# Expert outputs scattered to the tokens' slots during the expert loop, and a re-ordered attention stage

## What is computed

```
# layer 1, feed-forward: 32 experts, the best 4 for each token, capacity C = 2*1024*4/32 = 256 rows each
flat_ids, flat_w = top-4 experts and weights of each token
pos   = rank of the row within its expert
buf   = zeros(E, C, D).at[expert, pos].set(x[tok], mode='drop')     # rows past the capacity are dropped
eo    = (silu(buf @ gate) * (buf @ up)) @ w2
out_slots = eo[expert, pos]           # a position past the end reads the expert's last row, C-1
routed    = zeros.at[tok].add(out_slots * w)
# layer 2, attention: 32 heads of width 8, q and k normalised, softmax(q k / sqrt 8) v
```

## Time and profile before

| | |
|---|---|
| median of 3 runs | 1113.56 us (1111.15 to 1117.43) |
| the profiled execution | 1113.5 us |
| its span, first to last instruction | 1111.7 us |
| mean granted clock of TensorE | 0.881 of 2.4 GHz |
| busy: PE, DVE, ACT, POOL | 881.0, 649.1, 513.7, 372.0 us |

### The profile page before, as it was taken

The page is one execution under the profiler, slowest core; times in us unless marked ns, Lnnn a source line. Parts: engine busy times, 40 slices in busy tenths (PEclk is TensorE's granted clock), DMA queues, the critical chain, the costliest instruction groups (busy, mean ns, idle before and its releaser), DMA issues. The chain is left out here.

```text
span 1111.7 us, 17091 instructions
## 1 busy us (share of the span) xinstructions
PE 881.0 (79%) x6296; PEld 549.6 (49%) x6296; DVE 649.1 (58%) x1333; ACT 513.7 (46%) x881; POOL 372.0 (33%) x334
## 2 busy tenths in 40 slices
PE   4784689995504888467899898977888899999997
PEld 2334445654303666344555454544545555555554
DVE  4968634448742877244543557854768665754443
ACT  2554533442202888223445854356345777533332
POOL 3977223331379000363023475210135432400000
PEclk9785599998656999777856999989989999999999
DMA  9422044421024888321002345210145544533332
GB/s 324 168 71 69 1 122 130 130 84 42 10 99 137 289 269 291 129 75 39 1 1 85 92 140 182 86 44 29 30 146 160 150 129 138 175 100 100 100 100 81
DMA packets 56798, 126.44 MB, mean 114 GB/s; under 512 B 6921, under 2 KB 18569, under 8 KB 56722
## 3 DMA queue, kind: packets, MB, share of 16 engines
q1 hardware_dynamic: 45442, 108.65, 31.4%
q0 software_dynamic: 3072, 8.39, 2.4%
q10 hardware_dynamic: 8208, 8.39, 2.2%
HBM read 82.90 MB, written 42.50 MB: 113 GB/s over the span
## 5 line engine op out<-in xcount | busy, mean ns | idle before, releaser
L1403 PE MATMUL ps<-turned_buf,wb 128*128 128x512 f16 x576 | 136.5, 388 | 7.5 <-POOL wb L741 7.5
L1403 PE MATMUL ps<-turned_buf,W 128*128 128x512 f16 x576 | 136.9, 389 | 6.4 <-POOL W L741 4.2
L2122 DVE SCALAR_TENSOR_TENSOR ctx_sb<-ps,ctx_sb 128x512 f32<-128x512 f32 x96 | 66.3, 691 | 118.8 <-PE ps L1403 75.7
L1009 ACT ACTIVATE ctxT<-ctx_sb 128x512 f16<-128x512 f32 x96 | 60.3, 629 | 113.9 <-DVE ctx_sb L2122 113.9
L738 POOL TENSOR_SCALAR W<-W 128x768 f32<-128x768 f32 x32 | 69.0, 2155 | 127.9 <-ACT wb L1021 75.7
L2129 DVE TENSOR_TENSOR ctxT<-ctx_sb,ctxT 128x512 f16<-128x512 f32 x96 | 68.3, 712 | 64.0 <-ACT ctxT L1009 63.6
L1001 ACT ACTIVATE ctx_sb<-ps 128x512 f32<-128x512 f32 x96 | 57.2, 596 | 85.6 <-PE ps L1403 85.3
L1403 PEld LDWEIGHTS ps<-turned_buf,wb 128*128 128x128 f16 x576 | 55.9, 100 | 71.4 <-POOL wb L741 9.1
L1403 PEld LDWEIGHTS ps<-turned_buf,W 128*128 128x128 f16 x576 | 55.9, 100 | 71.3 <-issue 7.6
L1346 PE MATMUL ps<-turned_buf,W 128*128 128x512 f16 x360 | 88.2, 399 | 2.4 <-issue 2.4
L1419 PE MATMUL ps<-wb,ctxT 128*128 128x256 f16 x576 | 71.7, 275 | 10.8 <-DVE ctxT L2129 6.6
(11 more groups left out here) (378 smaller groups left out, 1800.6 us busy)
## 6 DMA issues: line engine op xcount, KB each, us to landing
W<-in_w SPq DMA_DIRECT2D x79, 384.0 KB, 3.7
kept<-W SPq DMA_DIRECT2D x24, 384.0 KB, 4.2
kept<-wb SPq DMA_DIRECT2D x24, 384.0 KB, 4.3
W<-kept SPq DMA_DIRECT2D x24, 384.0 KB, 3.0
wb<-kept SPq DMA_DIRECT2D x24, 384.0 KB, 3.1
seats<-wq ACTq DMA_DIRECT2D x1, 8192.0 KB, 37.8
arena<-seats SPq DMA_DIRECT2D x32, 256.0 KB, 3.8
served<-arena SPq DMA_DIRECT2D x32, 256.0 KB, 2.7
```

The costliest lines, as they stand in the source:

```text
L1009: nc.scalar.activation(h_16[:, g % 2, 0, :], h_g[:, g % 2, :], ACT.Copy).then_inc(sem("h_hi"), 1)
L1403: last = nc.tensor.matmul(bank(4 + n), w4[k % 4][:, w, n * D + c * P:n * D + (c + 1) * P], x16[:, i, c, half * HALF:(half + 1) * HALF], st ...
L2122: nc.vector.scalar_tensor_tensor(h_g[:, g % 2, :], bank(5), 1.0 / WSCALE, h_s[:, g % 2, :], ALU.mult, ALU.mult).then_inc(sem("gated"), 1)
```

## The change

1. `seats` rows get 32 more columns (ROW = 288), and the normalised rows are scattered with them. VectorE writes there, for each token and expert, a number from which the row's slot (token, order among its four) follows: a running count (`m_cum`) plus the partition's base, times "has a seat".
2. During the expert loop POOL reads from `e_x` the column of expert k, makes slot numbers `m_dest`, waits for `e_y(k)` and scatters its 256 rows with two indirect DMAs into `slots` (4096 rows in DRAM). SP's loads of rows wait for `e_dest` as well. SP no longer stores the outputs; it copies each expert's last row to `last_rows`.
3. After the loop SP loads `slots` with 8 plain DMAs into four buffers `e_back`. What had no seat is added by one more product per tile: the transposed weights of those picks (`over_T`) times `last_rows`.
4. The diagonals move from POOL to VectorE. `seats` and `slots` are set to zero later, by two DMAs from ScalarE's queue behind the conversion of the router's weights.
5. Before unit 0 all four sums and two pairs' queries are made, on more PSUM banks; pairs 2 and 3 follow at n = 3 and 11. 32 dummy products stand before the first sum, and one in each of the units 13 to 41.
6. FIRST_UNIT is 42, with three half steps per four units (18 beside the units, 14 behind), and the preparation of layer 2's experts moves ahead accordingly. q2_norm fuses two operations into one, three times.

The diff, cut to its core:

```diff
+ROW = D + E1
+SLOTS = T * TOP1
...
-        xn = sb("xn", [P, B, D])
+        x_rows = sb("xn", [P, B, ROW])
+        xn = x_rows[:, :, 0:D]
...
-        bkv3 = sb("bkv3", [1, 2 * D])
+        bkv3 = wq2[0:1, :, :].rearrange("p k d -> p (k d)")
...
-        seats = nc.dram_tensor("seats", (E1 * CAPACITY, D), F32, kind="Internal").ap()
-        served = nc.dram_tensor("served", (E1 * CAPACITY, D), F32, kind="Internal").ap()
+        seats = nc.dram_tensor("seats", (E1 * CAPACITY, ROW), F32, kind="Internal").ap()
+        slots = nc.dram_tensor("slots", (SLOTS, D), F32, kind="Internal").ap()
...
-        e_x = ar.take([3, CT, D])
+        m_w = ar.take([B, TOP1])
+        m_dest = ar.take([3, CT]).bitcast(U32)
+        e_x = ar.take([3, CT, ROW])
...
-        ar.at = at_back = ARENA - (2 * TOP1 * D + 2 * B * TOP1)
-        e_back = ar.take([2, TOP1, D])
-        m_from = ar.take([B, TOP1]).bitcast(U32)
-        m_w = ar.take([B, TOP1])
+        ar.at = at_back = ARENA - 4 * TOP1 * D
+        e_back = ar.take([4, TOP1, D])
...
-        FIRST_UNIT = 50
+        FIRST_UNIT = 42
+        REST = (8 * B + 2 - FIRST_UNIT) * 3 // 4
+        Q_TURN = (3, 11)
+        Q_PRODUCT = (4, 12)
+        Q_NORM = (1, 8, 19)
+        Q_SCALE = (2, 9, 20)
+        Q_LOW = (3, 5, 10, 13, 21, 23)
...
+        def steps_at(n):
+
+            return range(max(n - FIRST_UNIT, 0) * 3 // 4, max(n + 1 - FIRST_UNIT, 0) * 3 // 4)
...
-            sp.wait_ge(sem("seats_zero"), 16)
+            sp.wait_ge(sem("kv_mm"), 2 * B)
...
                 if k >= 3:
                     sp.wait_ge(sem("e_turn"), k - 2)
+                    sp.wait_ge(sem("e_dest"), k - 2)
                 sp.dma_start(e_x[:, k % 3, :, :], seats[k * CAPACITY:(k + 1) * CAPACITY, :].rearrange("(p c) d -> p c d", c=CT))\
...
-            def expert_store(k):
+            def last_row(k):
 
                 sp.wait_ge(sem("e_y"), k + 1)
-                sp.dma_start(served[k * CAPACITY:(k + 1) * CAPACITY, :].rearrange("(p c) d -> p c d", c=CT), e_y[k % 3])\
-                    .then_inc(sem("served", k % 3), 16)
+                sp.dma_start(last_rows[k:k + 1, :], e_y[k % 3][P - 1:P, CT - 1, :]).then_inc(sem("last", k % 3), 16)
+
+            def back(t):
+
+                if t >= 4:
+                    sp.wait_ge(sem("back_read"), t - 3)
+                sp.dma_start(e_back[:, t % 4, :, :].rearrange("p i d -> p (i d)"),
+                             slots.rearrange("(p k) d -> p (k d)", p=P)[:, t * TOP1 * D:(t + 1) * TOP1 * D])\
+                    .then_inc(sem("back", t % 4), 16)
...
-                        expert_store(k - 2)
+                        last_row(k - 2)
                 for k in range(E1 - 2, E1):
-                    expert_store(k)
+                    last_row(k)
+                for i in range(3):
+                    sp.wait_ge(sem("last", i), 16 * len(range(i, E1, 3)))
+                    sp.wait_ge(sem("served", i), 16 * CT * len(range(i, E1, 3)))
+                for t in range(B):
+                    back(t)
...
-            nc.gpsimd.memset(wq2[:, 0, :], 0.0).then_inc(sem("set_up"), 1)
...
+                nc.gpsimd.memset(k_norm[:, 0:2, :, :].rearrange("p k b h -> p (k b h)"), 0.0).then_inc(sem("set_up"), 1)
...
-            pool.wait_ge(sem("seats_zero"), 16)
+            pool.wait_ge(sem("seats_zero"), 16 * 2)
             pool.wait_ge(sem("seat"), 2)
             for t in range(B):
                 for i in range(TOP1):
                     nc.gpsimd.indirect_dma_start(seats, bass.IndirectOffsetOnAxis(ap=m_to[:, t, i:i + 1], axis=0),
-                                                 x_rms[:, t, :], None, bounds_check=E1 * CAPACITY - 1, oob_is_err=False)\
+                                                 x_rows[:, t, :], None, bounds_check=E1 * CAPACITY - 1, oob_is_err=False)\
                         .then_inc(sem("seated"), 16)
-            pool.wait_ge(sem("seat"), 4)
-            pool.wait_ge(sem("a1_pv"), 2)
-            for t in range(B):
-                for i in range(TOP1):
-                    ins = nc.gpsimd.tensor_scalar(diag(t, i), ident[:, :], m_w[:, t, i:i + 1], None, ALU.mult)
-            ins.then_inc(sem("back_diag"), 1)
-            for i in range(3):
-                pool.wait_ge(sem("served", i), 16 * len(range(i, E1, 3)))
-            for t in range(B):
-                if t >= 2:
-                    pool.wait_ge(sem("back_read"), t - 1)
-                for i in range(TOP1):
-                    nc.gpsimd.indirect_dma_start(e_back[:, t % 2, i, :], None, served,
-                                                 bass.IndirectOffsetOnAxis(ap=m_from[:, t, i:i + 1], axis=0),
-                                                 bounds_check=E1 * CAPACITY - 1, oob_is_err=False)\
-                        .then_inc(sem("back", t % 2), 16)
-                    if i == 1 and t in (2, 5):
-                        inv_sqrt_pair(t // 2 - 1 if t == 2 else 1)
+            for k in range(E1):
+                pool.wait_ge(sem("ex_in", k % 3), 16 * (k // 3 + 1))
+                if k >= 3:
+                    pool.wait_ge(sem("served", k % 3), 16 * CT * (k // 3))
+                nc.gpsimd.tensor_scalar(m_dest[:, k % 3, :], e_x[:, k % 3, :, D + k], -1.0, NOWHERE, ALU.mult, ALU.add)\
+                    .then_inc(sem("e_dest"), 1)
+                pool.wait_ge(sem("e_dest"), k + 1)
+                pool.wait_ge(sem("e_y"), k + 1)
+                for c in range(CT):
+                    nc.gpsimd.indirect_dma_start(slots, bass.IndirectOffsetOnAxis(ap=m_dest[:, k % 3, c:c + 1], axis=0),
+                                                 e_y[k % 3][:, c, :], None, bounds_check=SLOTS - 1, oob_is_err=False)\
+                        .then_inc(sem("served", k % 3), 16)
+            inv_sqrt_pair(0)
+            inv_sqrt_pair(1)
             inv_sqrt_pair(2)
             inv_sqrt_pair(3)
-            inv_sqrt(5, halves=(0,))
...
+            for k, sl in ((12, slice(0, 3)), (13, slice(3, 4))):
+                pool.wait_ge(sem("ln_var"), k + 1)
+                nc.gpsimd.tensor_tensor(rstd[:, sl], veps[:, sl], mhalf[:, sl], ALU.pow).then_inc(sem("ln_rstd"), 1)
...
-            act.wait_ge(sem("set_up"), SET_UP["zeros"])
-            nc.scalar.dma_start(seats.rearrange("(j p) d -> p j d", p=P),
-                                wq2[:, 0, :].unsqueeze(1).to_broadcast((P, E1 * CAPACITY // P, D))).then_inc(sem("seats_zero"), 16)
...
                 if k >= 3:
-                    act.wait_ge(sem("served", k % 3), 16 * (k // 3))
+                    act.wait_ge(sem("served", k % 3), 16 * CT * (k // 3))
+                    act.wait_ge(sem("last", k % 3), 16 * (k // 3))
...
+            act.wait_ge(sem("set_up"), SET_UP["zeros"])
+            no_rows = k_norm[:, 0:2, :, :].rearrange("p k b h -> p (k b h)")
+            nc.scalar.dma_start(seats.rearrange("(j p) d -> p j d", p=P),
+                                no_rows[:, 0:ROW].unsqueeze(1).to_broadcast((P, E1 * CAPACITY // P, ROW))).then_inc(sem("seats_zero"), 16)
+            nc.scalar.dma_start(slots.rearrange("(j p) d -> p j d", p=P),
+                                no_rows[:, 0:D].unsqueeze(1).to_broadcast((P, SLOTS // P, D))).then_inc(sem("seats_zero"), 16)
...
+            def turn_over():
+
+                pe.wait_ge(sem("w_ready"), 2)
+                pe.wait_ge(sem("shared_read"), 1)
+                for t in range(B):
+                    last = nc.tensor.transpose(ps[0:E1, 6 + t // 4, (t % 4) * S:(t % 4 + 1) * S], m_eq[:, t, :], ident[:, :])
+                last.then_inc(sem("w_turn"), 1)
...
             def sum_back(p):
 
-                if p:
-                    pe.wait_ge(sem("back_added"), p)
-                else:
+                if p == 0:
                     pe.wait_ge(sem("back_diag"), 1)
+                    pe.wait_ge(sem("wT_half"), 4)
+                    pe.wait_ge(sem("e_y"), E1)
+                    for i in range(3):
+                        pe.wait_ge(sem("last", i), 16 * len(range(i, E1, 3)))
                 for t in (2 * p, 2 * p + 1):
-                    pe.wait_ge(sem("back", t % 2), 16 * TOP1 * (t // 2 + 1))
+                    o = ps[:, sum_bank(p), (t % 2) * D:(t % 2 + 1) * D]
+                    nc.tensor.matmul(o, over_T[:, t * S:(t + 1) * S], last_rows, start=True, stop=False)
+                    pe.wait_ge(sem("back", t % 4), 16 * (t // 4 + 1))
                     for i in range(TOP1):
-                        last = nc.tensor.matmul(ps[:, 4, (t % 2) * D:(t % 2 + 1) * D], diag(t, i), e_back[:, t % 2, i, :],
-                                                start=(i == 0), stop=(i == TOP1 - 1))
+                        last = nc.tensor.matmul(o, diag(t, i), e_back[:, t % 4, i, :], start=False, stop=(i == TOP1 - 1))
                     last.then_inc(sem("back_read"), 1)
...
+            keep_busy(32, 3)
             sum_back(0)
+            sum_back(1)
             turn_x(0)
             queries(0)
-            sum_back(1)
+            sum_back(2)
```

(76 more changed lines are left out.)

179 lines of the change are left out of this document (109 added, 70 removed).

## The result

The changed kernel takes 1217.89 us (median of 4 runs, 1216.51 to 1224.46); the kernel before took 1114.48 on the same chip (median of 4). The ratio is 1.094, with a 95% interval of 1.089 to 1.099. Slower was right; 1150 was far too little, and 1217.9 lies outside the range of 1105 to 1195. The kernels of the experiments ran in three groups on three chips, so kernels of different groups are compared by their ratio to the kernel before, whose median beside them was 1112.3 to 1114.1 us. One execution of the kernel before, out of 25 beside the last group, took 1745.7 us; it counts as slow and is in no ratio.

The account below looks back on a forecast made before the run. It took the changed expert loop to be bound by a ring of waits through POOL's scatters and the row loads. 1113.5 - 5 + 5 + 1 + 70 - 4 - 30 = 1150.5, said as 1150 us; range 1105 to 1195.

Parts of the forecast that it names:

- the stage of 28 experts: Expert loop, a sign of being right: 28 experts would take some 155 us.
- Start, -5: Kernel start: zeros no longer go out with the first loads, so first transposes wait less; -5 us (0 to -6).
- The zeros, +5: First FFN: zeroing 13.6 MB beside it shares the DMA engines with its loads; +5 us (0 to +12).
- Seats, +1: Seating: two more VectorE operations on 128x256 between seat and m_to; +1 us.
- The ring, +58: Expert loop: row loads wait for POOL's destinations, behind earlier scatters; 10.6 us circle per two experts; +58 us (+48 to +68).
- The rival of a short, hidden ring: Expert loop: the circle is short and all hides, experts grow by 10 or so; 1090 us, chance 0.15.
- the one of POOL locked out by VectorE: Expert loop: each of two scatters waits for a VectorE weight split, 25 us more; 1175 us, chance 0.05.
- The clock in the loop, +12: Expert loop: at a clock of about 0.8, a third of the products' doubling at 1.2 GHz is added; +12 us.
- To the first unit, -4: Last expert to first attention unit: plain loads replace gathers, 33 us in place of 37.4; -4 us (-9 to +3).
- Units 0 to 41, -30: Second attention ahead of layer 2's tiles: fewer units, dummies added, 72 us for 102.3; -30 us (-14 to -43).
- Units 42 to 65, 0: Units beside layer 2's tiles: 63 us at most with 18 half steps, then 14 steps for 16; nothing (-5 to +5).
- TensorE falls to 1.2 GHz in the experts' gaps and stays there in the units: Expert loop and units: 36 us more instead of 12, units give only 19; 1185 us, chance 0.13.

Follow-up runs that it names:

- ring_three: The changed kernel with POOL making the destinations of expert k+1 before the scatters of expert k; 1148.26 us, ratio 1.032.
- no_over: mended without the eight products that add each expert's last row to the token sums; 1101.02 us, ratio 0.989.
- mended: The changed kernel with the edits of zeros_split and late_row together and no dummy products among the units; 1102.82 us, ratio 0.991.
- tempo_50: mended with layer 2's first expert tile at unit 50 and one half step per unit (16 beside 16 units); 1106.45 us, ratio 0.995.
- tempo_48: mended with layer 2's first expert tile at unit 48 and one half step per unit (18 beside 18 units); 1103.97 us, ratio 0.991.
- zeros_split: The changed kernel with the 4 MB zeroing transfer behind the first FFN and the 9 MB one behind that FFN's first two tiles; 1200.26 us, ratio 1.079.
- late_row: The changed kernel with destinations made two experts ahead and each expert's last-row store one round later in SP's order; 1129.10 us, ratio 1.015.

## Why the prediction was wrong in size

The direction and the main mechanism, the ring, were right. Against the profiled execution 66.0 us are missing (1216.5 for 1150.5): 15.8 at the start, 15.7 in the expert loop, 11.1 ahead of the first unit, 15.3 in the units and 8.1 behind the first tile. By its own signs the clock in the loop and the first transpose before 12 us came out; the stage of 28 experts took 177 us and not 155, and the unit stretch was over the 84 us that it had named as a sign of being wrong. By its own steps:

- **Start, -5: right.** 11.02 for 16.02.
- **The zeros, +5: the step that failed first.** The traffic was sized well (6.7 us). What was missed is the queue: the step counted the bytes on the DMA engines and gave nothing to ScalarE, which issues them. Before the change the same kind of transfer stood first in its program with nothing behind it in need. 13.9 us net, 21.0 at the issue. The profile before could not show it, with one such transfer, issued in 0.43 us. The Trainium skill ("Perfetto Trace Analysis", "DMA Instruction — HWDGE (DVE, Sync)") says that the span shown for a transfer is its sequencer's, until all descriptors are written, and that their buffer can fill. The trace agrees in that the span grew with what stood ahead, 21.01 us for the second right behind the first and 0.37 for it alone; that a full buffer was what held it, and how much fits, no run here shows.
- **Seats, +1: right** (16.8 + 4.6 - 20.6 = 0.8).
- **The ring, +58: right.** The first turn that must wait, turn(4), was put 17.1 us behind the first one (364.6 - 347.5) and came 17.2 behind (381.5). The rival of a short, hidden ring fell. So did the one of POOL locked out by VectorE: a scatter takes 0.99 us in the loop, on average. ring_three, which only lengthens the ring to three experts, gave the time that the ring's length gives.
- **The clock in the loop, +12: too small.** It was taken as 0.8 and applied to a third of the ring's products, 0.9 us a ring. The clock was 0.78, but the low share lay just on the ring: 12.6 us per ring from turn(4) at 381.5 to turn(30) at 545.6, 2.0 over the 10.6 of the high clock. 13 rings make 26, not 12; with the 58 and the 2.4 us by which turn(5) came later than forecast, the 85.7 are explained to 1 us. A mean clock is no guide where the slow pieces are the ones that all wait for: in the ring shown above, the turn and the gate/up right after the 5 us gap are the ones at the low clock.
- **To the first unit, -4: wrong sign.** The eight products for the tokens without a seat were in none of the terms; they are 6.2 us in no_over. POOL was also behind: at the end it had four experts' scatters in line, and the last ended at 565.4 us, 6.6 behind the last output copy (558.8), where 2.3 were forecast. The first sum so came 12.2 us behind that copy and not 8.9. These two make 9.5 of the 11.1 us, by sum and not by a run: mended, with a shorter line on POOL (4.7 us), started its first sum 1.4 us sooner after its last turn but its first unit no sooner. The rest is open.
- **Units 0 to 41, -30: half of it.** The sum had two values, 84 at the old clock and 59 at the high one, and took the middle, though no row showed that dummies raise the clock. The clock was 0.65, before it was 0.67, and the stage 87.6. Its own pieces give 80 with the dummies at the high clock and 87 with them at the low one, and the second is near what came. The dummies were costed at 7 or, at the low clock, 14; what they cost on balance is 6.8, since they kept 0.65 where 0.56 is had without them. That pays for a part of themselves only.
- **Units 42 to 65, 0: missed by 8.** 56 x 18/16 = 63 scaled the stretch with its steps, but it has 24 units in place of 16; it took 67.7. With 16 or 18 units there (tempo_50, tempo_48) the 8 us are gone.

The rival "TensorE falls to 1.2 GHz in the experts' gaps and stays there in the units" is nearest to what happened to the clock, and its 1185 would have been the better forecast. What it lacks is 16 us at the start, most of it the held queue that no case had, 11 ahead of the first unit and 8 beside tiles, less 4 by which it put loop and units too dear (it had 2.8 us more per ring and a gain of 19 in the units; 2.0 and 14.7 came).

## What to carry to other kernels

When a buffer gets a second reader, draw the circle through every queue that the release passes, and divide its length by the number of items in it; then do the same for the next queue, as here POOL's order hid SP's. Here the loop gave back 88.7 us (186.1 to 97.4) by making eight bytes per partition two rounds earlier and storing a row one round later. A large transfer was not free here for the engine that issued it with another large one just ahead in its queue, so give such a pair different places. And a filler product has a price at both clocks: count it against the time it is to save before it is put in.

## What the runs showed that was not expected

- ScalarE was held 21.0 us in issuing 4 MB 0.4 us behind 9 MB; 0.40 us for 9 MB and 0.37 for 4 MB, when 91 us apart (zeros_split: at 153.6 and 245.1).
- POOL's scatter starts 0.58 to 0.83 us after what it waited for, even where that is its own 0.2 us operation; with the destinations made ahead its round of two scatters and one set of destinations is 3.15 us (late_row).
- The units ahead of the tiles ran at a granted clock of 0.55 to 0.70 in all changed kernels with TensorE 87 to 91% busy, while the expert loop of mended, 83% busy, had 0.97.
- Executions of mended lay between 1094.7 and 1111.1 us, with granted clocks of 0.878 to 0.894; the kernel before, beside them on the same chip, stayed within 1109.3 to 1117.9 (17 runs).
